# Right-half column sums by accumulating transfers and four fp32 matmuls, a rearranged start, and VectorE's transposes from unit 5 on

## The chip, the cores and the metric

The kernel runs on one core of one Trainium2 chip. The metric is the device time of one execution in microseconds (us); lower is better. The profile is of one execution, and its times count from the start of the span.

## The reference

`x` is 128 samples of 64 channels by 1024. A small network on `cond_128` (two gelu layers, a softmax over 8) gives each sample a mixture `att`, and from it a 64x64 matrix and a bias:

```python
agg_w = einsum('bk,koi->boi', att, weight)      # 128 matrices of 64x64
agg_b = att @ bias_k                            # 128x64
y     = einsum('boi,bih->boh', agg_w, x) + agg_b[:, :, None]
# the layer on y (rows of 1024), added to x:
logits = y @ W_router.T                         # 8 experts, the two largest kept
h      = y @ A.T ; hw = h * combine             # 8 experts x rank 16
out    = x + y @ W_base.T + b_base + 2 * (hw @ B)
```

## The kernel before

W is the 1160-column matrix of A (128 columns), the router (8) and W_base (1024), transposed, in four blocks B11, B12, B21, B22 (two halves of the 1024 rows, two halves of 580 columns). Mixing and the product with W are exchanged: the kernel first forms Z = x @ W and then mixes Z with the 128x128 block-diagonal of two `agg_w` matrices. So the bias `agg_b` enters as `agg_b` times the column sums of W; these are needed for all 1160 columns before the first result. A unit is two tiles of 128 rows; there are 32 units, and each is a 2x2 block product in seven products (Winograd's form of Strassen's method) with weight sums T1 to T4 and input sums S1 to S4. Unit 0 uses eight plain products, because the T's are not ready. Each product is 24 matmuls of 290 columns: operands are split into a high and a low fp32r part (`x_hi`, `x_lo`, `w_hi`, `w_lo`), and high*high, high*low and low*high are added. ScalarE makes the high parts and copies out of PSUM, VectorE the low parts, sums, routing and results, GpSimd issues the transfers that add x to the result tile (`add_x`, with `accum_op`), and SyncE issues all other transfers. All engines follow orders written out by hand and meet at semaphores.

The start, in TensorE's order: the products of unit 0 with B11 and B21; `aggregate(0)`, which forms half of `agg_w`; A11\*B12; `aggregate(1)`; A12\*B22; a small fp32 matmul for `agg_b` (L505, into bank 4); the column sums of B11 and B21, 32 matmuls with a matrix of ones (L445, L446); A21\*B12; the column sums of B12, 16 matmuls; A22\*B22; those of B22, 16 matmuls; the mixing of unit 0's upper tile (L453 to L457); and then unit 1 with A11, A12 and so on. The sums of all four blocks use banks 6 and 7, and ScalarE copies them out (`column_sum`, L744) in two halves, before the mixing's third piece may overwrite bank 6.

VectorE's order there is: low part of B12, low of B22, T1, z11's low part, S1 and S3, the copy of `agg_b` out of PSUM (L1078), low of T1, A11's low part, T2, z12's low, T4, low of T2, A12's low, S2, T3, then `put_biases(0, 0)` (L1027, waits for both halves of the column sums, for `bias_out` and for `agg_w_out`), then `z21_low` (L962), for which TensorE waits before unit 1's A12. ScalarE's order is `aggregated(0)`, z11's high, `aggregated(1)`, high of T1, z12's save, A11's high, first half of the column sums, and at the end z22's save, second half, `b_hi` (waits for the transfer `bT_in`), `z21_high` (L723), high parts of S2 and S1.

SyncE's queue after the weights: unit 1's x; then, when all of `agg_w` has been copied out, four small `mix` loads, the 2 MB store of `agg_w` (L379), `bias_out` (L380), and after the landing of that store `bT` (L384).

In the units, `experts` multiplies the routed 128x128 matrix `hw`, transposed, with B. The upper tile's is transposed on TensorE (L502). The lower tile's is transposed on VectorE from unit 2 on, in 16 instructions of 32x32 (`transpose_lower`, L1009); in unit 1 TensorE does it (`first`). At the end of a unit VectorE waits for the store of an earlier tile (`stored[1]`) before S2 of the next unit (L941) and `put_biases`; `z21_low` follows. Units 1 and 2 are written out, units 3 to 30 are a loop of two units a turn, and unit 31 has its own order.

Of the kernel before, what the change touches and what calls it, by code (L numbers as in the profile page):

```python
# [7 lines left out]
ALU = mybir.AluOpType  # L8
# [72 lines left out]

BLOCK, BLOCKS = 32, 4
GROUP_COLS = CH * CH // GROUPS
MIX_COLS = GROUP_COLS + P
# [17 lines left out]
def build(nc, x, xT, small, keep, mix_w, wide, b_base, bT, out):  # L102
# [8 lines left out]
    with ExitStack() as ctx:  # L111
# [3 lines left out]
        def sem(name):  # L115
            return ctx.enter_context(nc.semaphore(name))
# [76 lines left out]
        b21_in = [sem("b21_in0"), sem("b21_in1")]  # L193
        b22_in = sem("b22_in")
        bT_in = sem("bT_in")
        bias_out_in = sem("bias_out_in")
# [107 lines left out]
        def acc(first):  # L304
            return ps[:, first:first + 2, 0:PART]
# [7 lines left out]
        def units(eng, unit, unit_1=None):  # L313

            if unit_1 is None:
                unit(1, 1, True)
            else:
                unit_1()
            unit(2, 2)
            with eng.Fori(0, (UNITS - 4) // 2) as turn:  # L320
                for i in range(2):
                    unit(turn * 2 + (3 + i), 1 + i)

# [17 lines left out]
        def _(sp):  # L341
# [29 lines left out]
            sp.dma_start(b12_sb[:], wide_blocks[1]).then_inc(b12_in, 16)  # L371
            sp.dma_start(b22_sb[:], wide_blocks[3]).then_inc(b22_in, 16)
            sp.wait_ge(x_lo_done, FIRST_SPLITS)
            load_xT(1)
# [13 lines left out]

            def unit(u, par, first=False):
# [21 lines left out]
        def _(pe):  # L411
# [92 lines left out]
            def chain(dst, stat, mov, done):  # L504
                nc.tensor.matmul(dst, stat, mov, start=True, stop=True).then_inc(done, 1)  # L505
# [79 lines left out]
            mixed(0, 1)  # L585
            pe.wait_ge(col_sum_done, 2)
            mixed(0, 2).then_inc(mixed_mm, 1)

            def unit(u, par, first=False):
                a, b = accumulators(par)  # L590
                pe.wait_ge(z12_summed, u)
                pe.wait_ge(x_lo_done, splits(u, "A11"))
                product(a, "A11", True)
                pe.wait_ge(z21_lo_done, u)
# [20 lines left out]
                product_part(a, "S3", 0, False)  # L615
                if first:
                    transpose_hw(u - 1, 1)
# [68 lines left out]
        def _(act):  # L686
# [16 lines left out]
            def lower_hwT_high(u):  # L703

                act.wait_ge(lower_hwT_made, u * (BLOCKS * BLOCKS))
                act.wait_ge(out_mm, tile_no(u, 1))
                nc.scalar.copy(hwT_hi[:], lower_hwT[:]).then_inc(hwT_hi_done, 1)
# [32 lines left out]

            def column_sum(half):
                act.wait_ge(col_mm, half + 1)
                cols = col_sum[:, half * HALF:(half + 1) * HALF].rearrange("p (k n) -> p k n", k=2)
                nc.scalar.copy(cols, acc(O_BANK + 2)).then_inc(col_sum_done, 1)  # L744

# [44 lines left out]
            save(sum2, b, z12_summed)  # L790
            act.wait_ge(xT_in, 16)
            x_high("A11")
            column_sum(0)
            for side in range(2):
                mix_high(0, side)
            z12_high(0)
            act.wait_ge(t_made, T_AT["T2"])
            split_weight(T2, t_stage)
            x_high("A12")
# [6 lines left out]
            def unit(u, par, first=False):  # L806
                a, b = accumulators(par)
                z21_high(u - 1, b)
                act.wait_ge(s_made, sums(u, "S2"))
                x_high("S2")  # L810
                x_high("S1")
                z22_high(u - 1)
# [4 lines left out]
                x_high("S3")  # L817
                hwT_high(1 if first else u + 1)
                if first:
# [14 lines left out]
                save(sum3, b, p5_saved)  # L834
                if first:
                    hwT_high(2)
                else:
                    lower_hwT_high(u - 1)
# [20 lines left out]
            x_high("S3")  # L859
            hwT_high(LAST + 1)  # L860
            act.wait_ge(s_made, sums(u, "S4"))
# [8 lines left out]
            z11_high(u)  # L870
            hwT_high(LAST + 2)
            act.wait_ge(product_mm, last_products("S3"))
# [3 lines left out]
            gate(u, 0)  # L876
            hwT_high(LAST + 3)
            act.wait_ge(z22_summed, u + 1)
# [4 lines left out]
            gate(u, 1)  # L883
            hwT_high(LAST + 4)

        @block.gpsimd
        def _(pool):
# [24 lines left out]

            def unit(u, par, first=False):
                mix_low(u, 0)
                mix_low(u, 1)
                add_x(u, 0)
                add_x(u, 1)
# [8 lines left out]
        def _(dve):  # L926
# [147 lines left out]
            dve.wait_ge(agg_b_mm, 1)  # L1074
            for par in range(PAIR):
                rows = slice(par * CH, (par + 1) * CH)
                of_tiles = ps[rows, O_BANK, 0:BATCH].rearrange("p (t par) -> p t par", par=PAIR)[:, :, par]
                nc.vector.tensor_copy(agg_b[rows, :], of_tiles).then_inc(agg_b_done, 1)  # L1078
            split_weight(T1, SPLIT_AT["T1"], t_stage)
            x_low(1, "A11")  # L1080
            dve.wait_ge(w_lo_done, SPLIT_AT["T1"])
            dve.wait_ge(t_made, T_AT["T1"])
            make_t(t_stage, b22_stage, t_stage)
            z12_low(0)
# [7 lines left out]
            dve.wait_ge(t_made, T_AT["T4"])  # L1092
            make_t(t_stage, b22_stage, b12_stage)
            dve.wait_ge(bias_out_in, 16)
            dve.wait_ge(agg_w_out, 16)
            dve.wait_ge(col_sum_done, 2)
            put_biases(0, 0)

            def unit_1():
# [3 lines left out]
                route(0, 0)  # L1103
                x_low(1, "S2")
# [3 lines left out]
                x_low(1, "S1")  # L1108
                z22_low(0)
# [35 lines left out]

            def unit(u, par):
                a, b = accumulators(par)
# [155 lines left out]
```

## Time and profile before

| | |
|---|---|
| time, median of 3 runs | 951.22 us (950.71 to 951.27) |
| the profiled execution's own time, and its span | 952.14 us, 950.17 us |
| TensorE busy | 943.1 us, 99% of the span |
| VectorE busy | 786.0 us, 83% |
| ScalarE, GpSimd busy | 330.6 us (35%), 89.8 us (9%) |
| mean granted TensorE clock | 0.999 |

A busy share that is near the whole span says that the order of that engine's instructions sets the time, and that what is taken from them or put between them shows in full, as long as nothing else makes that engine wait.

### The profile page before, as it was taken

How to read it: one execution, taken by the hardware profiler on the slowest of the kernel's cores; microseconds unless marked ns; L12 is line 12 of the kernel's file. 1: busy time of each engine (PE TensorE's matmuls, PEld its weight loads, DVE VectorE, ACT ScalarE, POOL GpSimd, SP SyncE). 2: the span in 40 equal slices, each digit the busy share in tenths (PEclk: the TensorE clock that was granted, in tenths of full speed). 3: DMA queues.
4: the chain of work that ended last, by engine and by line, in shares of the span. 5: the costliest groups of instructions: out<-in, count | busy, mean ns of one | idle time of the engine just before them, and what ended most of it. 6: DMA issues, size and time to landing. Idle time of an engine off the chain costs nothing.

```text
span 950.2 us, 19258 instructions
## 1 busy us (share of the span) xinstructions
PE 943.1 (99%) x6716; PEld 936.2 (99%) x6716; DVE 786.0 (83%) x2018; ACT 330.6 (35%) x671; POOL 89.8 (9%) x139
## 2 busy tenths in 40 slices
PE   9999999999999999999999999999999999999997
PEld 8999999999999999999999999999999999999997
DVE  4999788878888888888888888888888888888886
ACT  6553242333332333332333333333332333323331
POOL 1011010101010101100000101010101010101010
PEclk9999999999999999999999999999999999999999
DMA  8444444344434344434344434344444444443434
GB/s 306 139 113 99 111 116 130 93 131 92 112 116 133 90 120 106 112 113 127 98 109 117 112 113 115 110 97 128 111 115 106 119 94 122 110 125 99 126 91 111
DMA packets 35186, 111.34 MB, mean 117 GB/s; under 512 B 13104, under 2 KB 13360, under 8 KB 30816
## 3 DMA queue, kind: packets, MB, share of 16 engines
q1 hardware_dynamic: 25792, 77.32, 22.2%
q0 software_dynamic: 9376, 33.78, 21.4%
q8 instruction: 11, 0.18, 0.1%
q14 instruction: 7, 0.06, 0.0%
HBM read 75.37 MB, written 35.65 MB: 117 GB/s over the span
## 4 chain that ended last, share of the span: by engine, by line
PE 94%; DVE 3%; DMA 1%; issue 1%; ACT 0%; SPq 0%; DVEq 0%
PE ps L419 24%; PE ps L421 24%; PE ps L423 24%; PE ps L479 9%; PE ps L455 3%; PE ps L453 3%; PE ps L457 3%; DMA xT_sb<-in_xT 1%; PE ps L502 1%; PE ps L445 0%; PE ps L446 0%; DVE x_sb L1027 0%; DMA result<-x_sb 0%; DVE lower_hwT L1009 0%; PE ps L505 0%
## 5 line engine op out<-in xcount | busy, mean ns | idle before, releaser
L419 PE MATMUL ps<-w_hi,x_hi 128*128 128x290 f32 x1544 | 460.5, 298 | 1.1 <-DVE z_lo L962 0.6
L421 PE MATMUL ps<-w_lo,x_hi 128*128 128x290 f32 x1544 | 457.8, 297 | 0.0
L423 PE MATMUL ps<-w_hi,x_lo 128*128 128x290 f32 x1544 | 456.8, 296 | 0.0
L419 PEld LDWEIGHTS ps<-w_hi,x_hi 128*128 128x128 f32 x1544 | 292.2, 189 | 4.0 <-issue 2.8
L423 PEld LDWEIGHTS ps<-w_hi,x_lo 128*128 128x128 f32 x1544 | 291.3, 189 | 0.0
L421 PEld LDWEIGHTS ps<-w_lo,x_hi 128*128 128x128 f32 x1544 | 291.2, 189 | 0.0
L688 ACT CAST x_hi<-xT_sb 128x512 fp32r<-128x512 f32 x186 | 115.5, 621 | 189.9 <-DVE xT_sb L945 166.3
L929 DVE TENSOR_TENSOR x_lo<-xT_sb,x_hi 128x512 fp32r<-128x512 f32 x186 | 127.0, 684 | 22.7 <-ACT x_hi L688 22.7
L906 POOL DMA_DIRECT2D x_sb<-in_x x64 | 55.5, 868 | 535.6 <-DVE x_sb L1027 535.6
L1009 DVE STREAM_TRANSPOSE lower_hwT<-hw 32x32 f32<-32x32 f32 x464 | 94.0, 202 | 13.6
L710 ACT COPY sum<-ps 128x580 f32<-128x580 f32 x96 | 61.6, 642 | 88.1 <-PE ps L423 88.1
L1027 DVE SCALAR_TENSOR_TENSOR x_sb<-col_sum,agg_b,bias_out 128x1024 f32<-128x1024 f32 x64 | 81.8, 1279 | 0.0
L419 PE MATMUL ps<-t_hi,x_hi 128*128 128x290 f32 x248 | 74.0, 298 | 0.0
L423 PE MATMUL ps<-t_hi,x_lo 128*128 128x290 f32 x248 | 73.9, 298 | 0.0
L421 PE MATMUL ps<-t_lo,x_hi 128*128 128x290 f32 x248 | 73.3, 296 | 0.0
L948 DVE TENSOR_TENSOR sum<-ps,sum 128x580 f32<-128x580 f32 x92 | 69.6, 757 | 1.7 <-PE ps L423 0.9
L718 ACT CAST z_hi<-sum 128x580 fp32r<-128x580 f32 x31 | 21.0, 679 | 138.7 <-DVE sum L948 138.7
L455 PE MATMUL ps<-z_hi,mix_lo 128*128 128x384 f32 x189 | 64.2, 340 | 0.0
L453 PE MATMUL ps<-z_hi,mix_hi 128*128 128x384 f32 x189 | 64.1, 339 | 0.0
L457 PE MATMUL ps<-z_lo,mix_hi 128*128 128x384 f32 x189 | 63.5, 336 | 0.0
L899 POOL TENSOR_TENSOR mix_lo<-mix,mix_hi 128x128 fp32r<-128x128 f32 x64 | 31.1, 486 | 301.6 <-ACT mix_hi L692 301.6
L1022 DVE TENSOR_TENSOR x_sb<-ps,x_sb 128x776 f32<-128x776 f32 x62 | 59.2, 955 | 0.0
(128 smaller groups left out, 1138.4 us busy)
## 6 DMA issues: line engine op xcount, KB each, us to landing
x_sb<-in_x POOLq DMA_DIRECT2D x64, 512.0 KB, 5.4
result<-x_sb SPq DMA_DIRECT2D x63, 512.0 KB, 2.7
xT_sb<-in_xT SPq DMA_DIRECT2D x31, 1024.0 KB, 4.8
w_stage<-in_wide SPq DMA_DIRECT2D x4, 580.0 KB, 8.1
b_sb<-in_wide SPq DMA_DIRECT2D x2, 1160.0 KB, 14.5
agg_w_rows<-agg_w SPq DMA_DIRECT2D x1, 2048.0 KB, 7.5
mix<-agg_w_rows SPq DMA_DIRECT2D x124, 16.0 KB, 3.2
xT_sb<-in_xT SPq DMA_DIRECT2D x1, 768.0 KB, 8.6
```

What stands on the lines that cost most here:

```text
L419: nc.tensor.matmul(dst, x_hi[:, s, rows], high[:, c, cols], start=first, stop=False, skip_group_check=True)
L421: nc.tensor.matmul(dst, x_hi[:, s, rows], low[:, c, cols], start=False, stop=False, skip_group_check=True)
L423: mm = nc.tensor.matmul(dst, x_lo[:, s, rows], high[:, c, cols], start=False, stop=last, skip_group_check=True)
L453: nc.tensor.matmul(dst, mix_hi[:, side, :], high[:, columns(k)], start=start, stop=False, skip_group_check=True)
L455: nc.tensor.matmul(dst, mix_lo[:, side, :], high[:, columns(k)], start=False, stop=False, skip_group_check=True)
L457: return nc.tensor.matmul(dst, mix_hi[:, side, :], low[:, columns(k)], start=False, stop=True, skip_group_check=True)
L479: mm = nc.tensor.matmul(ps[:, banks[k], at], stat[:], mov[:, res], start=False, stop=True, skip_group_check=True)
L688: nc.scalar.copy(x_hi[:, SLOT[name], :], raw(name)).then_inc(x_hi_done, 1)
L929: nc.vector.tensor_tensor(x_lo[:, SLOT[name], :], raw(name), x_hi[:, SLOT[name], :].bitcast(F32), ALU.subtract).then_inc(x_lo_done, 1)
L948: nc.vector.tensor_tensor(dst[:], acc(first), dst[:], ALU.add).then_inc(done, 1)
L1009: nc.vector.transpose(lower_hwT[there, here], hw[here, there]).then_inc(lower_hwT_made, 1)
L1027: nc.vector.scalar_tensor_tensor(x_sb[:, side, :], col_sum[:, AR:WIDE], agg_b[:, bass.ds(tile_no(u, side), 1)], bias_out[:], ALU.mult, ALU.add
```

## The change

1. Column sums. Those of B12 and B22 (32 fp32r matmuls) go. In their place SyncE loads the first two chunks of B12 into `col_sum` after the weights; GpSimd then adds the other chunks of B12 and of B22 by three transfers with `accum_op`, each of which waits for the one before. Four fp32 matmuls of 290 columns with the ones matrix then add the two halves of `col_sum` over the partitions, into banks b and b+1. TensorE waits for the last of the transfers before them. Both `column_sum` copies on ScalarE follow them.
2. Order. The `agg_b` matmul goes to bank 7, and A21\*B12 right behind it, ahead of the column sums of B11 and B21. ScalarE copies `agg_b` in VectorE's place. VectorE makes T1 before the low part of B22; ScalarE makes T1's high part before `aggregated(1)`; the `mix` high parts come behind T2. Both parts of S2 and S1 of unit 1 are made before the column sums' copies and `put_biases(0, 0)`. Unit 1's A11 now also waits for the second copy.
3. Units 2, 3 and 4 are written out, and in them (as in unit 1) TensorE transposes the lower tile's `hw`; VectorE's transposes begin in unit 5. The loop covers units 5 to 30.

```diff
+BLOCKS_FROM = 5
@@ units
-            unit(2, 2)
-            with eng.Fori(0, (UNITS - 4) // 2) as turn:
+            for u in range(2, BLOCKS_FROM):
+                unit(u, 2 - u % 2, False, True)
+            with eng.Fori(0, (UNITS - 1 - BLOCKS_FROM) // 2) as turn:
                 for i in range(2):
-                    unit(turn * 2 + (3 + i), 1 + i)
+                    unit(turn * 2 + (BLOCKS_FROM + i), 1 + i)
@@ SyncE, after the load of B22
+            sp.dma_start(col_sum[:], wide_blocks[1][:, 0:WIDE]).then_inc(col_first_in, 16)
@@ GpSimd, after mix_w
+            pool.wait_ge(col_first_in, 16)
+            pool.dma_start(col_sum[:], wide_blocks[1][:, WIDE:2 * WIDE], accum_op=ALU.add).then_inc(col_in, 16)
+            pool.wait_ge(col_in, 16)
+            pool.dma_start(col_sum[:], wide_blocks[3][:, 0:WIDE], accum_op=ALU.add).then_inc(col_in, 16)
+            pool.wait_ge(col_in, 32)
+            pool.dma_start(col_sum[:], wide_blocks[3][:, WIDE:2 * WIDE], accum_op=ALU.add).then_inc(col_in, 16)
@@ TensorE
-            chain(ps[:, O_BANK, 0:BATCH], mix_w_sb[0:KERNELS, GROUP_COLS:MIX_COLS], attT[0:KERNELS, :], agg_b_mm)
+            chain(ps[:, T_BANK, 0:BATCH], mix_w_sb[0:KERNELS, GROUP_COLS:MIX_COLS], attT[0:KERNELS, :], agg_b_mm)
+            first_product(O_BANK, "A21", B12, True)
             pe.wait_ge(ones_done, 1)
+            pe.wait_ge(agg_b_done, 2)
             column_sums(O_BANK + 2, B11, start=True)
             column_sums(O_BANK + 2, B21, stop=True)
-            pe.wait_ge(agg_b_done, 2)
-            first_product(O_BANK, "A21", B12, True)
-            pe.wait_ge(col_sum_done, 1)
-            column_sums(O_BANK + 2, B12, start=True)
             first_product(O_BANK, "A22", B22, False)
-            column_sums(O_BANK + 2, B22, stop=True)
+            pe.wait_ge(z12_summed, 1)
+            pe.wait_ge(col_in, 48)
+            for part in range(2):
+                for c in range(2):
+                    at = c * HALF + part * PART
+                    mm = nc.tensor.matmul(ps[:, b + part, 0:PART], ones_r[:].bitcast(F32), col_sum[:, at:at + PART],
+                                          start=c == 0, stop=c == 1)
+            mm.then_inc(col_mm, 1)
@@ ScalarE
-            aggregated(1)
             act.wait_ge(t_made, T_AT["T1"])
             split_weight(T1, t_stage)
+            aggregated(1)
...
+            (agg_b copies, from VectorE)
...
-            column_sum(1)
+            act.wait_ge(s_made, sums(1, "S2"))
+            x_high("S2")
+            x_high("S1")
+            column_sum(0, O_BANK + 2)
+            column_sum(1, b)
@@ VectorE
             split_weight(B12, SPLIT_AT["B12"], b12_stage)
-            split_weight(B22, SPLIT_AT["B22"], b22_stage)
             make_t(t_stage, b12_stage, b11_stage)
+            split_weight(B22, SPLIT_AT["B22"], b22_stage)
...
+            x_low(1, "S2")
+            x_low(1, "S1")
             dve.wait_ge(bias_out_in, 16)
             dve.wait_ge(agg_w_out, 16)
+            dve.wait_ge(agg_b_done, 2)
             dve.wait_ge(col_sum_done, 2)
             put_biases(0, 0)
@@ VectorE, unit
-                transpose_lower(u - 1)
-                hwT_low(u - 1, 1, lower_hwT[:])
+                if early:
+                    hwT_low(u - 1, 1)
+                else:
+                    transpose_lower(u - 1)
+                    hwT_low(u - 1, 1, lower_hwT[:])
```

## Rows read from the trace of the kernel before

**Rows 1.** The page: busy time of each engine, its share of the span and instructions.
```profile
PE 943.1 (99%) x6716; PEld 936.2 (99%) x6716; DVE 786.0 (83%) x2018; ACT 330.6 (35%) x671; POOL 89.8 (9%) x139
```

**Rows 2.** The page: the chain that ended last, by engine.
```profile
PE 94%; DVE 3%; DMA 1%; issue 1%; ACT 0%; SPq 0%; DVEq 0%
```

**Rows 3.** Windows of the start: us; busy PE, PEld, DVE, ACT, POOL; clock; DMA.
```profile
40.01:42.15 2.14, 2.14 (x18) 2.14 (x17) 2.14 (x1) 1.32 (x2) 0.00 (x0) 1.00 0.66 232
42.15:45.35 3.20, 3.20 (x26) 3.20 (x25) 3.20 (x4) 0.00 (x0) 0.00 (x0) 1.00 0.70 187
45.35:47.50 2.15, 2.15 (x18) 2.15 (x17) 2.15 (x3) 0.64 (x1) 0.00 (x0) 1.00 0.00 0
47.50:49.09 1.59, 1.59 (x12) 1.58 (x11) 1.59 (x2) 1.39 (x2) 0.00 (x0) 1.00 0.00 0
```

**Rows 4.** TensorE's groups by shape in 0:50; an fp32 matmul counts as two instructions.
```profile
L505 PE MATMUL ps<-mix_w_sb,attT 8*128 8x512 f32 x16 | 2.3, 640 | 0.0
...
L505 PE MATMUL ps<-small_sb 128*128 128x128 f32 x2 | 0.4, 272 | 0.0
```

**Rows 5.** TensorE's timeline: fp32 matmul for agg_b, a transpose, a wait (start, us).
```profile
31.94 0.48 PE L505 MATMUL ps<-attT,mix_w_sb 8*128 8x128 f32 x2
32.36 0.40 PE L445 MATMUL ps<-w_hi,ones_r 128*128 128x290 f32 x1
32.60 0.29 PE L446 MATMUL ps<-w_lo,ones_r 128*128 128x290 f32 x1
...
53.90 0.27 PE L502 MATMUL ps<-keep_sb,hw 128*128 128x128 f32 x1
...
54.14 0.30 PE L421 MATMUL ps<-w_lo,x_hi 128*128 128x290 f32 x1
...
110.70 0.40 PE L419 MATMUL ps<-w_hi,x_hi 128*128 128x290 f32 x1 [0.61 <-DVE z_lo L962]
```

**Rows 6.** The issues of transfers in 0:110: count, size, median us to landing.
```profile
x_sb<-in_x POOLq DMA_DIRECT2D x5, 512.0 KB, 5.5
...
agg_w_rows<-agg_w SPq DMA_DIRECT2D x1, 2048.0 KB, 7.5
...
x_sb<-in_bT SPq DMA_DIRECT2D x1, 512.0 KB, 3.9
```

**Rows 7.** SyncE's queue, timeline.
```profile
41.31 0.33 SPq L384 DMA_DIRECT2D x_sb<-in_bT  x1
...
101.47 0.34 SPq L359 DMA_DIRECT2D result<-x_sb  x1
```

**Rows 8.** ScalarE's timeline.
```profile
22.64 2.13 ACT L733 CAST w_hi<-b_sb 128x2320 fp32r<-128x2320 f32 x1 [0.89 <-DMA b_sb<-in_wide]
```

**Rows 9.** VectorE's timeline of the start and of unit 2.
```profile
24.81 2.58 DVE L1034 TENSOR_TENSOR w_lo<-b_sb,w_hi 128x2320 fp32r<-128x2320 f32 x1 [1.85 <-ACT w_hi L733]
...
49.96 0.76 DVE L962 TENSOR_TENSOR z_lo<-ps,z_hi 128x580 fp32r<-128x580 f32 x1 [0.19 <-ACT z_hi L723]
...
92.89 3.71 DVE L1009 STREAM_TRANSPOSE lower_hwT<-hw 32x32 f32<-32x32 f32 x16
...
108.00 0.69 DVE L941 TENSOR_TENSOR xT_sb<-s_sb,xT_sb 128x512 f32<-128x512 f32 x1 [2.46 <-issue]
```

**Rows 10.** Two of VectorE's groups by shape in 20:50 (count, busy, mean ns, idle before).
```profile
L929 DVE TENSOR_TENSOR x_lo<-xT_sb,x_hi 128x512 fp32r<-128x512 f32 x2 | 1.4, 681 | 0.0
...
L1078 DVE COPY agg_b<-ps 64x64 f32<-64x64 f32 x2 | 0.4, 222 | 0.6 <-PE ps L505 0.6
```

**Rows 11.** Windows of one unit each, from one unit's upper experts to the next's.
```profile
84.80:114.66 29.86, 29.07 (x208) 1.00 0.48 119
114.66:143.63 28.97, 28.97 (x207) 1.00 0.41 108
201.42:230.04 28.62, 28.62 (x207) 1.00 0.43 111
```

More of the change, by code:

```diff
@@ L194, in build @@
         b22_in = sem("b22_in")
+        col_first_in = sem("col_first_in")
+        col_in = sem("col_in")
         bT_in = sem("bT_in")
@@ L315, in units @@
             if unit_1 is None:
-                unit(1, 1, True)
+                unit(1, 1, True, True)
             else:
                 unit_1()
-            unit(2, 2)
-            with eng.Fori(0, (UNITS - 4) // 2) as turn:
+            for u in range(2, BLOCKS_FROM):
+                unit(u, 2 - u % 2, False, True)
+            with eng.Fori(0, (UNITS - 1 - BLOCKS_FROM) // 2) as turn:
                 for i in range(2):
-                    unit(turn * 2 + (3 + i), 1 + i)
+                    unit(turn * 2 + (BLOCKS_FROM + i), 1 + i)
         LAST = UNITS - 1
@@ L387, in _, with unit @@
             load_mix(1, 1)
-            def unit(u, par, first=False):
+            def unit(u, par, first=False, early=False):
                 store(u - 1, 0)
@@ L585, in _, with unit @@
             mixed(0, 1)
-            pe.wait_ge(col_sum_done, 2)
+            pe.wait_ge(col_sum_done, 1)
             mixed(0, 2).then_inc(mixed_mm, 1)
-            def unit(u, par, first=False):
+            def unit(u, par, first=False, early=False):
                 a, b = accumulators(par)
@@ L592, in unit @@
                 pe.wait_ge(x_lo_done, splits(u, "A11"))
+                if first:
+                    pe.wait_ge(col_sum_done, 2)
                 product(a, "A11", True)
@@ L615, in unit @@
                 product_part(a, "S3", 0, False)
-                if first:
+                if early:
                     transpose_hw(u - 1, 1)
@@ L703, in lower_hwT_high @@
             def lower_hwT_high(u):
-                act.wait_ge(lower_hwT_made, u * (BLOCKS * BLOCKS))
+                act.wait_ge(lower_hwT_made, u * (BLOCKS * BLOCKS) - (BLOCKS_FROM - 2) * (BLOCKS * BLOCKS))
                 act.wait_ge(out_mm, tile_no(u, 1))
@@ L739, in aggregated, with column_sum @@
                     nc.scalar.copy(agg_w[:, at:at + BANK], ps[:, O_BANK + r, :]).then_inc(agg_done, 1)
-            def column_sum(half):
-                act.wait_ge(col_mm, half + 1)
+            def column_sum(half, bank):
+                act.wait_ge(col_mm, 2)
                 cols = col_sum[:, half * HALF:(half + 1) * HALF].rearrange("p (k n) -> p k n", k=2)
-                nc.scalar.copy(cols, acc(O_BANK + 2)).then_inc(col_sum_done, 1)
+                nc.scalar.copy(cols, acc(bank)).then_inc(col_sum_done, 1)
             act.wait_ge(att_step, 1)
@@ L785, in _ @@
             z11_high(0)
-            aggregated(1)
             act.wait_ge(t_made, T_AT["T1"])
             split_weight(T1, t_stage)
+            aggregated(1)
             act.wait_ge(product_mm, FIRST_PRODUCT["A12", B22])
             save(sum2, b, z12_summed)
+            act.wait_ge(agg_b_mm, 1)
+            for par in range(PAIR):
+                rows = slice(par * CH, (par + 1) * CH)
+                of_tiles = ps[rows, T_BANK, 0:BATCH].rearrange("p (t par) -> p t par", par=PAIR)[:, :, par]
+                nc.scalar.copy(agg_b[rows, :], of_tiles).then_inc(agg_b_done, 1)
             act.wait_ge(xT_in, 16)
             x_high("A11")
-            column_sum(0)
-            for side in range(2):
-                mix_high(0, side)
             z12_high(0)
@@ L798, in _ @@
             split_weight(T2, t_stage)
+            for side in range(2):
+                mix_high(0, side)
             x_high("A12")
@@ L801, in _, with unit @@
             save(sum3, O_BANK, z22_summed)
-            column_sum(1)
+            act.wait_ge(s_made, sums(1, "S2"))
[3 more added lines that the diff above has]
+            column_sum(1, b)
             act.wait_ge(bT_in, 16)
             nc.scalar.copy(b_hi[:], bT_stage).then_inc(b_hi_done, 1)
-            def unit(u, par, first=False):
+            def unit(u, par, first=False, early=False):
                 a, b = accumulators(par)
                 z21_high(u - 1, b)
-                act.wait_ge(s_made, sums(u, "S2"))
-                x_high("S2")
-                x_high("S1")
+                if not first:
+                    act.wait_ge(s_made, sums(u, "S2"))
+                    x_high("S2")
+                    x_high("S1")
                 z22_high(u - 1)
@@ L817, in unit @@
                 x_high("S3")
-                hwT_high(1 if first else u + 1)
+                hwT_high(2 * u - 1 if early else u + (BLOCKS_FROM - 1))
                 if first:
@@ L834, in unit @@
                 save(sum3, b, p5_saved)
-                if first:
-                    hwT_high(2)
+                if early:
+                    hwT_high(2 * u)
                 else:
@@ L859, in _ @@
             x_high("S3")
-            hwT_high(LAST + 1)
+            hwT_high(LAST + (BLOCKS_FROM - 1))
             act.wait_ge(s_made, sums(u, "S4"))
@@ L870, in _ @@
             z11_high(u)
-            hwT_high(LAST + 2)
+            hwT_high(LAST + (BLOCKS_FROM - 1) + 1)
             act.wait_ge(product_mm, last_products("S3"))
@@ L876, in _ @@
             gate(u, 0)
-            hwT_high(LAST + 3)
+            hwT_high(LAST + (BLOCKS_FROM - 1) + 2)
             act.wait_ge(z22_summed, u + 1)
@@ L883, in _ @@
             gate(u, 1)
-            hwT_high(LAST + 4)
+            hwT_high(LAST + (BLOCKS_FROM - 1) + 3)
         @block.gpsimd
@@ L911, in _, with unit @@
             add_x(0, 1)
-            def unit(u, par, first=False):
+            def unit(u, par, first=False, early=False):
                 mix_low(u, 0)
@@ L1073, in _ @@
             make_s3(1)
[L1074 to L1078, printed above, removed]
             split_weight(T1, SPLIT_AT["T1"], t_stage)
+            dve.wait_ge(w_lo_done, SPLIT_AT["T1"])
+            make_t(t_stage, b22_stage, t_stage)
             x_low(1, "A11")
-            dve.wait_ge(w_lo_done, SPLIT_AT["T1"])
-            dve.wait_ge(t_made, T_AT["T1"])
-            make_t(t_stage, b22_stage, t_stage)
             z12_low(0)
@@ L1103, in unit_1 @@
                 route(0, 0)
-                x_low(1, "S2")
                 dve.wait_ge(b_hi_done, 1)
@@ L1107, in unit_1 @@
                 hwT_low(0, 0)
-                x_low(1, "S1")
                 z22_low(0)
@@ L1144, in unit_1, with unit @@
                 put_biases(1, 1)
-            def unit(u, par):
+            def unit(u, par, first=False, early=False):
                 a, b = accumulators(par)
@@ L1163, in unit @@
                 x_low(u, "A22")
-                transpose_lower(u - 1)
-                hwT_low(u - 1, 1, lower_hwT[:])
+                if early:
+                    hwT_low(u - 1, 1)
+                else:
+                    transpose_lower(u - 1)
+                    hwT_low(u - 1, 1, lower_hwT[:])
                 dve.wait_ge(stored[0], u * 16)
```

## The prediction

> **What bounds the kernel now.** I read the page first. TensorE is busy for 99% of the span, the next engine, VectorE, for 83% [rows 1], and the chain that ended last is TensorE's for 94% [rows 2]. A share over the whole span hides the stages, so I then took windows of the start, where most of the change lies. [...] So from 40 to 49 us TensorE's order of work is the bound and VectorE is close behind it: VectorE has no gap worth naming before z21_low at 49.96 [rows 9], for which TensorE waits only when A11 of unit 1 is done, 3.2 us after 49.09 (a product takes 3.20 [rows 3]), at 52.3. VectorE's result is there at 50.7, 1.6 us early. Last I read units as windows. A settled unit is 28.62 us; unit 2's window is 29.86 and unit 3's 28.97, so 1.24 and 0.35 above it [rows 11]. The waiting matmul behind them is at 110.70 with 0.61 us of idle, for z21_low [rows 5].
>
> **The column sums, TensorE.** Removed are two groups of 16 matmuls, 2.14 and 2.15 us [rows 3]: 4.29 us, all of it on the path, as nothing else runs on that engine. This is 0.134 us a matmul.
> Added are four fp32 matmuls of 290 columns, eight instructions. No row has this shape. An fp32 instruction of 128 columns lasts 272 ns and one of 512 lasts 640 [rows 4]: 0.958 ns a column, so 427 ns at 290. Of this some 166 ns is the way through the array that the next one overlaps (an L419 matmul lasts 300 ns and the next starts 134 ns behind it), which leaves 0.26 us an instruction. [...] So 1.93 to 2.10 us; I take 2.0. Entering and leaving fp32 costs something too: from the fp32 matmul at 31.94 to the second one behind it at 32.60 are 0.66 us [rows 5], of which two instructions at 0.11 and one at 0.134 explain 0.35; so 0.3 us. Sum 2.3 us, bounds 2.0 and 2.5. TensorE alone gains 4.29 - 2.3 = 2.0 us.
>
> **The column sums, transfers.** TensorE asks for the last accumulating transfer when A22\*B22 is done. The B11 and B21 sums and A21\*B12 only change places, so this is 45.35 less the 2.14 of the B12 sums: 43.2 us. The first plain transfer follows that of B22, which ScalarE sees land at 22.64 [rows 8]; with 594 KB (half of that one) at the rate at which the start's queue moves (B12 and B22 share it), I put it 1.4 us later, at 24.1. GpSimd is free then. Each accumulating transfer of 524 KB lands 5.5 us after its issue [rows 6]; ours have 13% more bytes, and as some 3 us of the 5.5 go with the bytes, I take 5.8 (bounds 5.5, if bytes cost nothing, and 6.2, if all of it scales). They are in series: issued at 24.1, 29.9 and 35.8, the last lands at 41.6 if nothing is in its way. Something is: the 2 MB store of agg_w. It lands 7.5 us after its issue [rows 6], and bT, which waits for that, is issued at 41.31 [rows 7], so it is issued at 33.8 now. With T1's high part ahead of aggregated(1) on ScalarE this becomes about 34.5, and it holds the transfer engines to about 41.2. If the third transfer has its bytes moved only after this, it needs its own 3 us from there: 44.2. I take 44.2, since the reverse is seen at 101.47, where a store issued while such an addition is under way comes in only behind it: VectorE waits for it until 108.00 [rows 7, 9], 6.5 us. So one DMA is done before the other is served. TensorE then stands for 1.0 us (bounds 0 and 3).
> [...]
>
> **What hides behind this, and what is late next.** GpSimd's queue: behind its third issue (35.8) stand the low parts of mix, which need ScalarE after T2 (about 37.5), and TensorE wants them at 45.5: cost nothing, and would cost only beyond 5 us of delay. SyncE's queue: one more issue of about 0.6 us before a wait that ends at 18: nothing. ScalarE: the copies of agg_b (0.22 us each on VectorE [rows 10]), S2 and S1 go into time in which it waits for A22\*B22: nothing. Both column sum copies now come behind the fp32 matmuls, 0.65 us each, while TensorE mixes for 1.59 us [rows 3]: hidden to about 0.1. VectorE: T1 moves into the 1.85 us in which it waited for B22's high part [rows 9], B22's low part ends 0.7 later, near 28.0, ahead of its product at 28.6. It loses the copy of agg_b with its wait (0.44 and 0.6) and does S2 and S1 earlier (2 by 0.60 us net of overlap, 681 ns each [rows 10]) while it would wait for the sums. put_biases then ends at about 49.3 and z21_low at 50.5. bT is issued when agg_w has landed (about 42) and lands after 3.9 [rows 6] plus up to 3 of the addition's bytes: 46 to 49; b_hi and z21_high stand behind it on ScalarE, so z21_low ends between 50.4 and 51.5. TensorE is at that point at 52.3 - 2.0 + 1.0 = 51.3. Nothing more is lost, but the start can't gain over 2.0 even if the addition were early.
> The start: 2.0 - 1.0 = 1.0 us gained.
>
> **The transposes.** Units 2, 3 and 4 each give TensorE one fp32 transpose. From one at 53.90 to the second matmul behind it, at 54.14, are 0.24 us [rows 5], against 0.134: 0.11 each, 0.3 in all, on the path. VectorE loses 3.71 us in each [rows 9]. What that is worth is not 3.71: the low part of hw^T now waits for TensorE's own transpose, in the middle of S3 (near 95.8 where the 16 transposes ended at 96.6), and the result that follows waits for the experts. I estimate the result 0.5 us earlier, GpSimd's addition 0.6 earlier, so the store at 101.47 and its landing (108.00) 0.5 to 0.9 earlier against TensorE. Units 2 and 3 have 1.24 + 0.35 = 1.6 us of excess; I take 1.3 of it back and leave 0.3. Units 2 to 4: 1.3 - 0.3 = 1.0 gained (bounds -0.3, all excess stays, and 1.3).
>
> **Sum.** 1.0 + 1.0 = 2.0 us. Against the profiled execution's own 952.14 this gives 950.1; that one was 0.9 above the median of 951.22, so for the median: 949.2 us, 0.21% less. A measurement of this kernel can tell about 0.2% (1.9 us) from no change, so this forecast stands on the edge of it.
>
> **The rivals.**
> - A: the third addition is off the path. It gets the engines at once, at 37.4, and lands by 43.2; the agg_w store waits instead, which only bT feels. For it: nothing says which of the two is served first when the store came first. Against it: the late store above. Then TensorE doesn't stand: 4.29 - 2.3 + 1.0 = 3.0 us, 948.2. [...]
> - B: units 2 to 4 give nothing. The excess there is the landing of a store behind an addition, and it comes up again in unit 2 or at the new loop entry at unit 5. Then 1.0 - 0.3 = 0.7, 950.5. For it: the wait at 108.00 is for a transfer, and no longer for the transposes. Against it: units 3 and 4 come within 0.35 with the same order.
> - C, slower: the additions are slower than the x tiles' because rows of 4640 bytes are handled as two pieces of up to 4096 bytes, each at the price of a whole one. The byte part (3 us) doubles to 6 and each transfer takes 8.5 us: 24.1 + 3 by 8.5 = 49.6 without the store in its way. TensorE stands 6.4 us: 951.2 - 2.0 + 6.4 - 1.0 = 954.6. Without a stand the whole gain is 3.0 us, so it decides once the last addition lands behind 43.2 + 3.0 = 46.2; slower by 1.9 us takes a landing behind 48.1. No row has a transfer with additions of over 4096 bytes a row, so I can't exclude it.
> - D: agg_w's store and bias_out are both served ahead of the third addition, which lands at 45.2 to 46.2. TensorE stands 2 to 3 us, the start gains 0 or loses 1.0, and with 1.0 from the units the time is 950.2 to 951.2. For it: bias_out is issued right behind the store. Against it: it is another transfer of the same queue, and in the late store above the queues took turns after one transfer.
>
> **Chances.** The forecast 0.40 (948.7 to 949.8), A 0.24, B 0.14, D 0.14, C 0.08. Faster by over 0.2% is below 949.3: half of the forecast's and nearly all of A's, with the rest of A's and a few of B and D at the edge: 0.47. Slower by over 0.2%: C, 0.07. Same: 0.46. The range takes in the forecast, A, B and D: 947.7 to 951.2; C is left out.
>
> **What would show it.** In the profile after: no L446 behind 43; eight fp32 instructions with 0.24 to 0.26 us between starts, ahead of them a wait of TensorE for a transfer that ends near 44.2 (A: none; D: 46; C: 50); the three additions' issues on GpSimd near 24, 30 and 36; unit 1's A11 at 48.1 instead of 49.09; unit windows 2 to 4 at 28.7 to 29.0; no L1009 before unit 5 and 48 of them fewer. What would make it wrong: the landing of the third addition above all, then a store in unit 2 that lands as late as now.

## The result, and the profile after

The changed kernel takes 956.36 us (median of 6 runs, 955.95 to 957.89) against 951.25 for the kernel before in the same measurement: a ratio of 1.0058, with a 95% interval of 1.0048 to 1.0068. It is slower by 5.1 us; 949.2 us, 2.0 faster, was forecast. The profiled execution is one of the longer ones, 957.89 us, with a span of 956.2.

The page of the changed kernel, the busy line, the granted clock and the chain that ended last:

```profile
PE 942.2 (99%) x6695; PEld 935.0 (98%) x6695; DVE 776.5 (81%) x1968; ACT 331.4 (35%) x673; POOL 93.8 (10%) x142
...
PEclk9989999999999999999999999999999999999999
...
PE 92%; DMA 5%; DVE 1%; issue 1%; SPq 0%; ACT 0%; DVEq 0%; ACTq 0%
```

Against [rows 1, 2]: TensorE's busy time is almost the same although 32 matmuls are gone, a transfer stands in the chain with 5%, and the third of the 40 slices has a lower clock. The waits of the start name the place:

```profile
ACT col_sum L757 <- PE ps L587: 9.5, 1, 9.5
DVE x_sb L1057 <- ACT col_sum L757: 9.2, 1, 9.2
...
PE ps L587 <- DMA col_sum<-in_wide: 7.3, 1, 7.3
POOL col_sum L925 <- DMA col_sum<-in_wide: 6.7, 1, 6.7
```

L587 is the first of the four fp32 matmuls. TensorE waited 7.3 us for the third addition. ScalarE, which copies the sums out, then waited for TensorE, and VectorE for ScalarE. The queues of GpSimd and SyncE show how the transfer came to be so late (start, length of the issue, the wait before it):

```profile
23.50 0.90 POOL L921 DMA_DIRECT2D col_sum<-in_wide  x1 [7.79 <-DMA col_sum<-in_wide]
29.53 0.86 POOL L923 DMA_DIRECT2D col_sum<-in_wide  x1 [5.13 <-DMA col_sum<-in_wide]
37.05 0.88 POOL L925 DMA_DIRECT2D col_sum<-in_wide  x1 [6.66 <-DMA col_sum<-in_wide]
```

```profile
33.99 0.79 SPq L384 DMA_DIRECT2D agg_w_rows<-agg_w  x1
34.83 1.93 SPq L385 DMA_DIRECT2D bias_out<-in_b_base  x1
44.11 0.33 SPq L389 DMA_DIRECT2D x_sb<-in_bT  x1
```

And the chain of 30 to 60 in order of time (start, us):

```profile
29.53 7.17 DMA col_sum<-in_wide
36.70 0.34 issue
37.05 13.42 DMA col_sum<-in_wide
50.47 0.14 issue
50.61 3.91 PE ps L587 x8
54.52 0.18 PE ps L458
```

The first addition takes 6.0 us from issue to issue of the next, the second 7.2 to its landing, the third 13.4. The packets in the trace say what the third did in that time: no packet of it starts before 42.5; until 41 nearly all packets are the 16 KB ones of agg_w's store, from 41 to 42.5 most are those of bias_out; 119 of the addition's 128 packets have ended by 47.2, and the last six end one after another from 47.6 to 50.0.

Where this late end comes from is not shown, but the times of the packets point at one transfer engine that was late already (the trace doesn't name the engines). All but three of the store's 128 packets have ended by 41.8, and the last one ends at 43.7; in the kernel before all have ended by 40.9. And the last three packets of the addition (starts at 48.61, 49.12, 49.64, 0.37 us each) stand in turn with packets of bT (48.95, 49.47, 49.99, 0.17 us each), which SyncE had issued at 44.11.

The windows from A22\*B22's end to unit 1's A11 (us, TensorE busy, granted clock):

```profile
43.13:47.21 4.08, 0.16 (x2) 1.00 0.99 224
47.21:50.61 3.40, 0.00 (x1) 0.51 0.32 102
50.61:54.03 3.42, 3.42 (x7) 0.50 0.01 2
54.14:56.10 1.96, 1.96 (x13) 1.00 0.00 0
```

TensorE had nothing to do from 43.3; from 47.2 to 54.0 the granted clock is 0.50, so the fp32 matmuls, which begin at 50.61, run at it. They take 3.53 us, from 50.61 to the start of the mixing at 54.14. Unit 1's A11 starts 6.85 us later than in the kernel before (first this kernel, then the one before):

```profile
55.94 0.32 PE L424 MATMUL ps<-w_hi,x_hi 128*128 128x290 f32 x1
```

```profile
49.09 0.30 PE L419 MATMUL ps<-w_hi,x_hi 128*128 128x290 f32 x1
```

The sum of the parts is 6.9: the 32 matmuls that are gone (-4.29), the wait (7.61 from start to start where 0.13 is normal: +7.48), the fp32 matmuls (+3.53) and a first mixing matmul of 0.39 where 0.17 is normal (+0.22). From there to the end 0.8 us comes back (the spans differ by 6.0).

### The profile page after: what moved, and what is told of

The parts are those of the page before. It is cut to its first block, busy times and chain, and to the rows that moved or that the text cites. A ratio compares the mean times of both kernels' runs of the same rounds, so it can differ in the third digit from the quotient of the medians.

```text
span 956.2 us, 19065 instructions
## 1 busy us (share of the span) xinstructions
PE 942.2 (99%) x6695; PEld 935.0 (98%) x6695; DVE 776.5 (81%) x1968; ACT 331.4 (35%) x673; POOL 93.8 (10%) x142
## 4 chain that ended last, share of the span: by engine, by line
PE 92%; DMA 5%; DVE 1%; issue 1%; SPq 0%; ACT 0%; DVEq 0%; ACTq 0%
PE ps L424 24%; PE ps L428 24%; PE ps L426 24%; PE ps L484 9%; DMA col_sum<-in_wide 5%; PE ps L460 3%; PE ps L458 3%; PE ps L462 3%; DMA result<-x_sb 1%; PE ps L507 1%; PE ps L587 0%; DVE lower_hwT L1039 0%; DVE x_sb L1057 0%; DVE sum L978 0%; DVE x_sb L1274 0%
## 5 line engine op out<-in xcount | busy, mean ns | idle before, releaser
L1039 DVE STREAM_TRANSPOSE lower_hwT<-hw 32x32 f32<-32x32 f32 x416 | 84.2, 203 | 12.2
```

The lines of the kernel that those rows point to most:

```text
L1039: nc.vector.transpose(lower_hwT[there, here], hw[here, there]).then_inc(lower_hwT_made, 1)
```

## The experiments

Each was measured beside the kernel before on its chip; times are medians.

**The third addition left out.** TensorE waits for two additions; the last two chunks of B22 are missing from the sums.

```diff
-            pool.wait_ge(col_in, 32)
-            pool.dma_start(col_sum[:], wide_blocks[3][:, WIDE:2 * WIDE], accum_op=ALU.add).then_inc(col_in, 16)
-            pe.wait_ge(col_in, 48)
+            pe.wait_ge(col_in, 32)
```

> The changed kernel without its third adding transfer; TensorE waits for two only, so the last two chunks of B22 are missing from the column sums and the output is not the reference's. Theory: the whole loss is TensorE's wait of 7.3 us for the third addition and what follows from it (the granted clock is at 0.5 behind the wait, and the eight fp32 instructions take 3.53 us there). The second addition landed at 36.7, 6.4 us before TensorE asks, so here there is no wait, the clock stays at 1.00, the eight instructions take 2.0 to 2.3 us, unit 1's A11 starts near 47.0 (56.10 in the changed kernel, 49.09 before), and the time is 951.25 - 2.1 - 0.5 = 948.7 us. Rival: fp32 matmuls of 290 columns take 3.5 us whatever the clock; then A11 starts near 48.3 and the time is 950.0.

948.68 us (before 951.53, ratio 0.9970, 0.9958 to 0.9982). The groups by shape, first of this run and then of the changed kernel (count, busy, mean ns, idle before):

```profile
L587 PE MATMUL ps<-col_sum,ones_r 128*128 128x290 f32 x8 | 2.1, 406 | 0.0
```

```profile
L587 PE MATMUL ps<-col_sum,ones_r 128*128 128x290 f32 x8 | 3.9, 664 | 7.3 <-DMA col_sum<-in_wide 7.3
```

And this run's window of the fp32 matmuls:

```profile
43.11:44.84 1.73, 1.73 (x10) 1.00 0.34 85
```

At a granted clock of 1.00 the same eight instructions go from 43.11 to 44.84, 1.73 us, and with the 0.2 us that the next matmul takes longer, 2.0. Unit 1's A11 starts at 46.65. So the wait and the clock behind it are the loss, and everything else in the change together makes the kernel about 2.8 us faster, with two chunks left out; as fp32r matmuls those would be 8 of the 32 that took 4.29, 1.1 us of TensorE.

**The additions alone with the engines.** The store of agg_w, and what follows it on SyncE, waits for the third addition.

```diff
+            sp.wait_ge(col_in, 48)
             sp.dma_start(agg_w_dram.rearrange("(b i) o -> b (i o)", b=BATCH), agg_w[:]).then_inc(agg_w_out, 16)
```

> The changed kernel with the store of agg_w (and what follows it on SyncE) held back until the third addition has landed. Theory: the third addition took 13.4 us only since it stood behind the store and bias_out; alone it takes 6 to 7 us as the first two did, lands at 43 to 44, and TensorE waits under 1 us there. The store then lands near 51, bT near 55, and TensorE waits instead at unit 1's A12, from 50.5 to 57, for z21_low behind b_hi: 955 to 957 us. Rival: the third addition is slow by itself (its engines or its rows), and TensorE waits at the column sums for over 5 us as before.

956.75 us (before 951.06). Its chain, 30 to 60:

```profile
36.53 5.96 DMA col_sum<-in_wide
42.50 7.27 DMA agg_w_rows<-agg_w
49.84 3.22 DMA x_sb<-in_bT
```

```profile
PE ps L425 <- DVE z_lo L993: 5.6, 1, 5.6
```

Issued half a microsecond earlier than in the changed kernel, the third addition lands after 5.96 us instead of 13.42. So neither its rows of 4640 bytes nor the adding make it slow; the traffic ahead of it and beside it does. GpSimd's own work behind the issue isn't the reason either: mix_lo's two instructions start at 37.70 and take 4.1 us in the changed kernel, and start at 37.32 and take 4.4 here. The price moves to the store and bT, and TensorE waits 5.6 us for z21_low: the start has one stretch of transfers too many, whichever goes first.

**bias_out behind bT.** The store alone stays ahead of the third addition.

```diff
-            sp.dma_start(bias_out[:], b_base.partition_broadcast(P)).then_inc(bias_out_in, 16)
             ...
             sp.dma_start(bT_stage, bT).then_inc(bT_in, 16)
+            sp.dma_start(bias_out[:], b_base.partition_broadcast(P)).then_inc(bias_out_in, 16)
```

> The changed kernel with bias_out issued behind bT instead of ahead of the third addition. In the changed kernel's trace the third addition's first packets start at 42.5, when bias_out's are mostly done and agg_w's have been done since 41. Theory: both transfers of SyncE's queue are served ahead of the addition; without bias_out it starts and lands 1.3 us earlier (128 packets at 0.16 us over 16 engines): 955.1 us. Rival: the addition waits for the 2 MB store alone, and the time stays at 956.4; or bT, now less disturbed, changes nothing, as it isn't waited for.

954.20 us (before 951.06, ratio 1.0031, 1.0020 to 1.0042); the seven runs spread from 951.74 to 955.39. Its chain:

```profile
35.63 11.26 DMA col_sum<-in_wide
47.03 2.19 PE ps L587 x8
```

The profiled execution is the fastest, 951.74. There the first packets of the addition start at 40.8, when most of agg_w's have ended, 1.7 us earlier than in the changed kernel, and it lands 3.6 earlier. TensorE waits 3.8 us, its granted clock stays at 1.00, and from the first fp32 matmul to the mixing are 1.8 us:

```profile
47.03 2.19 PE L587 MATMUL ps<-col_sum,ones_r 128*128 128x290 f32 x8 [3.82 <-DMA col_sum<-in_wide]
48.84 0.55 PE L458 MATMUL ps<-z_hi,mix_hi 128*128 128x384 f32 x1
```

So bias_out did go ahead of the addition, and moving it is worth 2.2 us in the median (954.20 against 956.36, each beside the kernel before). The late end is there too: the last six packets of the addition start one after another from 44.5, and the last ends at 46.6.

**The wait filled.** 56 fp32r matmuls into the same banks ahead of the wait.

```diff
+            for _ in range(56):
+                nc.tensor.matmul(ps[:, b, 0:PART], ones_r[:], w_hi[:, B11, 0, 0:PART], start=True, stop=True)
             pe.wait_ge(col_in, 48)
```

> The changed kernel with 56 more matmuls with the ones matrix (fp32r, 290 columns, 7.5 us at 0.134) ahead of the wait for the third addition, into the banks that the column sums then start afresh. Theory: the clock stays at 1.00 through the wait, the eight fp32 instructions take 2.0 to 2.3 us instead of 3.53, and the time falls by 1.3 to 1.5 us to about 955.0, as the addition still lands near 50.5. Rival: the fp32 instructions are as slow at the full clock, and the time stays at 956.4. Second rival: the fillers delay the wait past the landing (43.1 + 7.5 = 50.6), which takes no more than 0.2 us.

955.80 us (before 951.53, ratio 1.0042, 1.0027 to 1.0058). The windows of the fillers and of the fp32 matmuls:

```profile
42.90:50.50 7.60, 7.60 (x59) 1.00 0.70 178
50.50:52.37 1.87, 1.87 (x10) 1.00 0.02 7
```

The clock stays at 1.00 and the fp32 matmuls take 1.8 us (1.9 in the window, which starts a little before them). The mixing starts at 52.37 where it was at 54.14 in the changed kernel's profile, 1.8 us sooner: that is what the lower clock cost there. The medians differ by less, 0.6 us (0.8 when each is taken against its own kernel before). The four runs lie within 0.4 us, those of the changed kernel within 1.9: the fillers end at 50.5 in every execution, and where the addition lands sooner than in the profiled one they hold TensorE up. That last step is argued, not measured.

**The transposes alone**, in the kernel before: the third part of the change as the diff shows it (units 2 to 4 written out, TensorE's transposes in them).

> The kernel before with the third part of the change alone: units 2 to 4 written out, TensorE transposes the lower tile in them. The prediction gave this 1.0 us (950.2). The trace of the changed kernel has six unit windows from unit 2 on that are only 0.5 us shorter together than those of before, with 0.9 us of excess in the first turn of the loop: by that the time is 950.7. Rival: the excess belongs to the loop's entry and VectorE's first transposes and only moves, so nothing is gained and three transposes are paid: 951.3 to 951.6.

952.04 us (before 951.53, ratio 1.0005, 0.9996 to 1.0014). Windows of unit 2 and unit 5 (28.62 is a settled unit):

```profile
84.68:113.66 28.98, 28.95 (x208) 1.00 0.47 121
171.10:201.24 30.14, 29.05 (x208) 1.00 0.39 103
```

Unit 2 is down to 0.4 us of excess and unit 5 has 1.5 us: it came up again behind, and three transposes are paid. The rival was right.

**Units written out, nothing else**, in the kernel before: VectorE's transposes still from unit 2, the loop from unit 5.

```diff
-            unit(2, 2)
-            with eng.Fori(0, (UNITS - 4) // 2) as turn:
+            for u in range(2, BLOCKS_FROM):
+                unit(u, 2 - u % 2)
+            with eng.Fori(0, (UNITS - 1 - BLOCKS_FROM) // 2) as turn:
```

> The kernel before with units 2 to 4 written out and nothing else: VectorE transposes from unit 2 on as before, the loop begins at unit 5. It tells where the long unit window comes from (29.86 for unit 2 in the kernel before, 30.14 for unit 5 with TensorE's transposes in units 2 to 4). Theory A, the loop's entry: window of unit 2 at 28.6 to 28.8, window of unit 5 at 29.2 or more, the time within 0.5 us of before. Theory B, the first unit in which VectorE transposes: the window of unit 2 stays at 29.8 and unit 5's is under 28.8.

951.39 us (before 951.12, ratio 1.0003, 0.9994 to 1.0012). Unit 2 and unit 3:

```profile
84.59:114.73 30.14, 29.08 (x207) 1.00 0.44 117
114.73:143.35 28.62, 28.62 (x208) 1.00 0.45 114
```

The long window stays with unit 2, the first unit in which VectorE transposes, and doesn't go with the loop's entry.

**The kernel before, a second profile**, unchanged.

> The kernel before, unchanged, for a second profile: the profiled execution of before took 952.14 us where the median is 951.2. If the 29.86 of unit 2's window is of that execution, this one has a shorter window there when its time is near 951.2; if it belongs to the kernel, it is at 29.5 to 30 again.

This execution took 951.14 us. Its units 2 and 3:

```profile
84.69:114.14 29.45, 29.07 (x208) 1.00 0.48 121
114.14:142.94 28.80, 28.80 (x208) 1.00 0.43 109
```

So the kernel has the long window, at 29.45 here and 29.86 in [rows 11]; a part of it differs from one execution to the next.

**The order alone.** The changed kernel with 32 fp32r matmuls in place of the transfers and the fp32 ones.

```diff
-            pe.wait_ge(col_in, 48)
-            for part in range(2):
-                for c in range(2):
-                    ...
+            column_sums(b, B12, start=True)
+            column_sums(b, B22, stop=True)
```

> The changed kernel with the column sums of B12 and B22 by 32 fp32r matmuls again (behind A22*B22, into bank b) and without the four transfers: the new order, T1, agg_b, S2 and S1 moved, and the transposes. Theory: the new order costs and gives nothing by itself, since TensorE has no wait in the start of either; the time is that of the transposes alone, 950.2 to 950.7. Rival: part of the loss is in the new order (mix high parts behind T2, both copies behind the sums, put_biases behind them): unit 1's A12 waits for z21_low, as both copies, b_hi and z21's parts now follow the last column sum at 47.4: z21_low would end at 50.9 against TensorE's 52.3, so this shows only if one of them is over 1.4 us later than worked out; then the time is over 951.3.

951.82 us (before 951.53, ratio 1.0002, 0.9993 to 1.0011), 0.2 us from the transposes alone. Unit 1's A11 starts at 49.07, where the kernel before has 49.09. The new order costs nothing that can be measured and by itself gives nothing.

**Two additions and eight fp32r matmuls.** The whole computation: the last two chunks of B22 by the fp32r way, ahead of the fp32 matmuls, which add to the same banks.

```diff
+            high, low = weight_parts(B22)
+            for part in range(2):
+                dst, cols = ps[:, b + part, 0:PART], slice(part * PART, (part + 1) * PART)
+                for c in range(2, CHUNKS):
+                    nc.tensor.matmul(dst, ones_r[:], high[:, c, cols], start=c == 2, stop=False,
+                                     skip_group_check=True)
+                    nc.tensor.matmul(dst, ones_r[:], low[:, c, cols], start=False, stop=False,
+                                     skip_group_check=True)
-            pe.wait_ge(col_in, 48)
+            pe.wait_ge(col_in, 32)
```

> The changed kernel with two adding transfers (the third left out) and, for the last two chunks of B22, eight fp32r matmuls ahead of the four fp32 ones: the whole computation. The second addition landed at 36.7, so TensorE doesn't wait. Against the run with two additions and nothing in place of the third (948.7 us, its fp32 matmuls 2.0 us) this adds 8 by 0.134 = 1.1 us: 949.8, 1.7 us under the kernel before. Rival: the fp32r sums push unit 1's z21_low or the copies late; then 950.5 or more.

949.25 us (before 951.06, ratio 0.9980, 0.9971 to 0.9989): 1.8 us faster, where 1.7 was expected. TensorE doesn't wait for the additions, and unit 1's A11 starts at 47.72.

**The same with VectorE's transposes from unit 2**, units 2 to 4 written out.

> The same with VectorE's transposes from unit 2 on, as in the kernel before, and units 2 to 4 still written out. Theory on the units: the first unit in which VectorE transposes pays once for a store that lands late (a window of 29.9 to 30.1 where the others have 28.6), wherever that unit is; TensorE's three transposes only move it from unit 2 to unit 5 and cost 0.32 us. Then here the long window is unit 2's, unit 5's is 28.6 to 28.9, and the time is 0.3 us under the run with transposes from unit 5: 949.5. Rival: the long window belongs to the entry of the loop, which stays at unit 5 here; then unit 5's window stays near 30 and the time is not below the other's.

948.97 us (before 951.06, ratio 0.9973, 0.9963 to 0.9984), 0.3 us less than the last. But the theory behind the number is not borne out: unit 2's window is 28.62 here, not 29.9.

**The same with the loop from unit 3**, so that only the start differs from the kernel before.

> The version with two additions and eight fp32r matmuls, VectorE's transposes from unit 2 on and the loop from unit 3 on, both as in the kernel before: only the start differs from the kernel before. If writing units out is worth nothing, this is within 0.3 us of the version with units 2 to 4 written out (948.97): 948.9. If the entry of the loop costs more when it comes early (unit 2's window 29.86 in the kernel before), it is 1 us slower than that, 950.

948.74 us (before 951.12, ratio 0.9976, 0.9967 to 0.9985). Units 2 and 3:

```profile
83.55:112.17 28.62, 28.62 (x207) 1.00 0.47 122
112.17:140.77 28.60, 28.60 (x207) 1.00 0.42 111
```

Neither has an excess. Part 3 of the change isn't needed. Unit 1's A11 starts at 47.83.

**VectorE in place of the third addition.** The chunks lie in SBUF already; VectorE adds them after T4, and TensorE has no fp32r matmuls for the sums. The units are as in the last run. Against the changed kernel:

```diff
-            pool.wait_ge(col_in, 32)
-            pool.dma_start(col_sum[:], wide_blocks[3][:, WIDE:2 * WIDE], accum_op=ALU.add).then_inc(col_in, 16)
             ...
+            dve.wait_ge(col_in, 32)
+            nc.vector.tensor_tensor(col_sum[:], col_sum[:], b22_sb[:, WIDE:2 * WIDE], ALU.add).then_inc(col_added, 1)
-            pe.wait_ge(col_in, 48)
+            pe.wait_ge(col_added, 1)
```

> As the last one, but VectorE adds the last two chunks of B22 (which lie in SBUF in fp32) to the sums of the two transfers, one tensor_tensor of 1160 columns, about 1.3 us, at 38.6, and the eight fp32r matmuls go. The whole computation. TensorE saves 8 by 0.134 = 1.07 us. VectorE waited 1.0 us for the copies ahead of put_biases(0, 0) (gap at 47.58 in the version with eight fp32r matmuls), so z21_low moves to about 49.9, when TensorE arrives at 49.9: 0.8 to 1.1 us faster, 947.9. Rival: VectorE's 1.3 us come out again as a wait of TensorE at A12, and nothing is gained.

947.55 us (947.29 to 949.43; before 951.12, ratio 0.9966, 0.9954 to 0.9978): 3.6 us faster than the kernel before, where the changed one was 5.1 slower. VectorE's timeline:

```profile
38.64 1.35 DVE L1110 TENSOR_TENSOR col_sum<-col_sum,b_sb 128x1160 f32<-128x1160 f32 x1
...
47.83 1.27 DVE L1055 SCALAR_TENSOR_TENSOR x_sb<-col_sum,agg_b,bias_out 128x1024 f32<-128x1024 f32 x1
49.15 0.76 DVE L990 TENSOR_TENSOR z_lo<-ps,z_hi 128x580 fp32r<-128x580 f32 x1
```

The addition took 1.35 us, and there is no gap left ahead of put_biases (L1055), which had 1.2 us in the last run; z21_low (L990) ends at 49.9, in time for TensorE, which needs it at 50.3. Unit 1's A11 starts at 47.08 and the windows of units 2 to 4 are 28.61 to 28.62.

## Why the prediction was wrong

- TensorE's side of the column sums: right. Removed 4.29 us; the fp32 matmuls were taken at 2.3 us (2.0 to 2.5) and take 2.0 at a granted clock of 1.00, 1.73 and the 0.2 that the next matmul takes longer. The 1.93 us at the low end of its range for the eight instructions (0.24 each) is a term that no run shows; in its place the runs showed the 1.73.
- TensorE asks at 43.2: it asked at 43.1. The first plain transfer at 24.1: the first addition was issued at 23.50. bT at about 42: it was issued at 44.11, as the store ahead of it took 10.0 us to its landing where 7.5 was taken.
- The step that failed is "I take 44.2" for the landing of the third addition, with "TensorE then stands for 1.0 us (bounds 0 and 3)". It landed at 50.5, 6.3 us later, and TensorE stood 7.5. The 6.3 are three terms:
  - Its first packets started at 42.5 where 41.2 was taken, because bias_out's went ahead of it as well: 1.3 us. That is the order of rival D, at D's price of 1 to 2 us.
  - From the first packets to the landing the prediction took 3 us. With the transfer engines to itself the addition takes 4.4 (38.1 to 42.5 in the run in which the store waits): 1.4 us.
  - In the traffic it took 8.0, which is 3.6 us more, with the late end of its last packets. For this the prediction had nothing, though the kernel before has such an end beside unit 2's store: of the 128 packets of the addition there, 124 have started by 104.6 and the last four start one by one between 105.0 and 106.0.
- The additions before it took 6.0 and 7.5 us from issue to issue where 5.8 was taken, so the third was issued at 37.05 and not at 35.8. This cost nothing more, as far as the runs show: with bias_out behind bT it was issued at 35.63, and its packets still waited for the store's, until 40.8.
- "One DMA is done before the other is served" was taken from the store issued at 101.47 [rows 7, 9], and the packets there show it nearly: the store's first starts at 104.47, when 120 of the addition's 128 have ended, and seven of the addition start behind it. From that the prediction took one transfer's turn. In the changed kernel the addition came behind two transfers of SyncE's queue, the store and bias_out, of 128 packets of 16384 and of 4096 bytes (its first packet is at 42.5; at 40.8 where bias_out wasn't there), while its last packets stand in turn with bT's one by one. By what rule an engine passes from one queue to the other is not shown.
- Rival A had the third addition get the engines at once. It didn't: issued at 37.05, it has its first packet at 42.5. Alone with the engines it took 5.96 us to its landing.
- The clock isn't in the prediction at all. It took TensorE's instructions as in windows in which TensorE never waits, where the granted clock is 1.00 [rows 3]. The fp32 matmuls behind the wait ran at 0.50 and took 3.53 us where they take 1.73 at 1.00: 1.8 us more. A wait of TensorE was priced at its length only.
- Together: the start was forecast to gain 1.0 us and lost 6.85 in the profile. Of these 7.9 us the wait is 6.5 (7.5 against 1.0) and the fp32 matmuls are 1.4 (3.53 and 0.22 against 2.3).
- Rival C put the slower outcome on rows cut in two. The outcome had its sign and nearly its time (954.6), not its mechanism: each addition has 128 packets of 4640 bytes, one a row, so no row was cut, and alone with the engines an addition takes 5.96 us where C had 8.5. That its price came so near is luck.
- "Nothing more is lost" on ScalarE and VectorE in the start: right. The order alone is within 0.3 us of the kernel before, and without the wait z21_low ended at 49.7 to 50.2, no later than forecast.
- Units 2 to 4, "1.0 gained": wrong; rival B was right. The transposes alone make the time 0.5 us higher in the median, with an interval from -0.04% to +0.14% that holds no gain of 0.1%. The windows of units 2 to 4 themselves came out as forecast or nearly so (28.72, 28.73 and 29.03 in the changed kernel); the excess is in unit 5 (29.52, and 30.14 with the transposes alone).

What is open is where the late end of the transfers comes from, and why unit 2's long window is there in three profiles that have 32 fp32r matmuls and VectorE's transposes from unit 2 (29.45, 29.86, 30.14), and not in three with the shorter start (28.62 each). In the first three the addition that runs beside unit 2's store takes 4.2 to 5.1 us from its first packet to its last, in the others 3.0 to 3.3. That doesn't explain it throughout: in the long unit 5 of the transposes alone it takes 3.0. An instruction load of 16 KB also falls between the addition's packets in the first three, and behind the last of them in the others. What of this makes the stall isn't shown. Unit 2's excess weighs nearly as much as the start's own gain: of the 3.6 us of the fastest version, 2.0 are there when unit 1's A11 starts (47.08 against 49.09), the rest comes in the units behind it.

## What to carry to other kernels

Work taken off the bounding engine and given to transfers is free only while the transfers' own chain ends in time: write down when each link is issued, and what else is in the queues in that stretch. Here two links fitted and the third met a 2 MB store; doing the third on VectorE, which could spare 1.35 us before its result was needed, gave what the whole change was after. A wait of TensorE costs more than its length when the clock falls in it: price the wait, and then the work behind it at the lower clock (here 3.53 us at 0.50 for 1.73 at 1.00, behind a wait of 7.3 us; behind one of 3.8 us the clock was still at 1.00).

## What wasn't expected of the hardware

- An adding transfer of 594 KB takes 5.96 us alone, and 13.42 behind a 2 MB store and a 524 KB broadcast that were issued on the other queue 3.1 and 2.2 us before it.
- TensorE's clock fell in the wait: it had no work from 43.3, the granted clock is 1.00 up to 47.2 and 0.50 from 47.2 to 54.0, and the fp32 matmuls began at 50.6. With 56 matmuls in the gap it stayed at 1.00. Eight fp32 instructions of 290 columns take 1.73 us from the first start to the next matmul's at 1.00 and 3.53 at 0.50.
- Beside other traffic a transfer's end can come long after the bulk of it: 119 of the addition's 128 packets had ended by 47.2, the last at 50.0. Alone with the engines the last ended 0.5 us behind the 119th (41.7 and 42.1).
